# A transformer block on eight cores: one stage's loop reordered by engine, its stores moved to another queue

## What is computed

```python
x = x + attn_a(ln(x))   # delta = softplus((xn @ W0.T) @ W_delta.T + b); prefix sum of delta*B1 over the rows
x = x + ffn(ln(x))      # xn @ W_eff.T + b
x = x + attn_b(ln(x))   # softmax attention over the 8192 rows of a batch
x = x + ffn(ln(x))

# attn_a, with h = ln(x) and sums over the whole sequence:
dA = jnp.exp(delta * A1) * B1
dB = jnp.cumsum(delta * B1, axis=1)
y = dA * sum(h * Cs) + dB * sum(Cs) + residual * D
```

## Time and profile before

| what | value |
|---|---|
| time, median of 2 runs | 7493.05 us (7473.88 to 7512.21) |
| the profiled execution: time of its run | 7213.63 us |
| the profiled execution: span of its slowest core | 7211.3 us |
| spans of the 8 cores | 7192.7 to 7211.3 us |
| busy over the span | PE 61%, ACT 35%, DVE 24%, POOL 18% |
| first x2 of the stage to the last | 1416.9 to 3435.7 us |

### The profile page before, as it was taken

One profiled execution on the slowest core, in us unless ns is written; L12 is line 12 of the kernel. 1 busy time (PEld: TensorE's weight loads), 2 busy tenths in 40 slices (PEclk: granted clock), 3 DMA queues, 4 the chain that ended last, 5 costly groups with the idle time before them and its releaser, 6 DMA issues.

```text
span 7211.3 us, 65380 instructions; the slowest of 8 cores (7192.7 to 7211.3 us)
## 1 busy us (share of the span) xinstructions
PE 4364.3 (61%) x20288; PEld 1955.4 (27%) x20288; DVE 1721.1 (24%) x2744; ACT 2500.9 (35%) x4418; POOL 1323.4 (18%) x611
## 2 busy tenths in 40 slices
PE   3788887122222222222679997998899855555555
PEld 1333333000000010010334443444444322222222
DVE  0222222122222222222002221332233122222221
ACT  0555554133333333333323332333333222222222
POOL 2222222444444444444000000000000000000000
PEclk9899998565656555555889999999999977777777
DMA  4222222422222111111211110221122111111110
GB/s 124 100 99 96 95 97 76 123 72 71 74 70 75 64 60 61 53 60 35 75 42 40 55 59 30 82 94 59 53 88 94 47 35 41 41 41 43 47 41 25
DMA packets 183210, 475.80 MB, mean 66 GB/s; under 512 B 51149, under 2 KB 51278, under 8 KB 182868
## 3 DMA queue, kind: packets, MB, share of 16 engines
q1 hardware_dynamic: 98740, 295.19, 13.0%
q10 hardware_dynamic: 84128, 176.45, 6.3%
HBM read 295.12 MB, written 176.42 MB: 65 GB/s over the span
## 4 chain that ended last, share of the span: by engine, by line
PE 49%; ACT 17%; DVE 12%; POOL 11%; issue 5%; DMA 3%; ACTq 1%; DVEq 0%; POOLq 0%; SPq 0%
PE PC L1026 13%; PE PA L933 6%; PE PB L933 6%; PE PB L712 5%; PE PA L873 4%; PE PB L892 3%; DVE st L191 3%; PE PA L420 3%; PE PC L1075 3%; PE PT L186 2%; POOL p2F L670 2%; POOL p2H L723 2%; POOL p2D L673 2%; POOL g_bf L451 2%; ACT L208 2%
## 5 line engine op out<-in xcount | busy, mean ns | idle before, releaser
L1026 PE MATMUL PC<-v_res,pt_sb 128*128 128x512 bf16 x4096 | 994.9, 405 | 285.7 <-ACT pt_sb L1013 280.4
L1087 POOL TENSOR_TENSOR s_out<-zs,x3b 128x1024 f32<-128x1024 f32 x32 | 75.0, 2342 | 3694.9 <-DVE zs L1082 3694.9
L186 PE MATMUL PT<-s_id,xn2b 128*128 128x128 bf16 x512 | 64.7, 306 | 1119.6 <-ACT xn2b L212 1119.6
L1026 PEld LDWEIGHTS PC<-v_res,pt_sb 128*128 128x128 bf16 x4096 | 416.5, 103 | 813.1 <-issue 411.8
L933 PE MATMUL PA<-kT_res,qT_t 128*128 128x512 bf16 x2048 | 470.7, 384 | 28.4 <-ACT P_bf L970 22.5
L933 PE MATMUL PB<-kT_res,qT_t 128*128 128x512 bf16 x2048 | 462.9, 379 | 0.0
L186 PEld LDWEIGHTS PT<-s_id,xn2b 128*128 128x128 bf16 x512 | 49.5, 137 | 1174.7 <-issue 1174.7
L712 PE MATMUL PB<-W_eff,xn2T 128*128 128x512 bf16 x1024 | 345.1, 511 | 1.6 <-DVE p2G L720 1.5
L451 POOL TENSOR_TENSOR g_bf<-delta_f,s_B1bc 128x1024 bf16<-128x1024 f32 x64 | 150.0, 2344 | 796.2 <-ACT delta_f L442 796.2
L723 POOL TENSOR_TENSOR p2H<-p2G,p2F 128x1024 f32<-128x1024 f32 x64 | 149.6, 2337 | 758.5 <-DVE p2G L720 758.5
L933 PEld LDWEIGHTS PA<-kT_res,qT_t 128*128 128x128 bf16 x2048 | 201.5, 99 | 277.5 <-issue 42.9
(11 more groups left out here) (164 smaller groups left out, 6837.3 us busy)
## 6 DMA issues: line engine op xcount, KB each, us to landing
sc_z<-zs ACTq DMA_DIRECT2D x96, 512.0 KB, 4.6
zl<-sc_z SPq DMA_DIRECT2D x96, 512.0 KB, 4.9
xb<-x SPq DMA_DIRECT2D x64, 512.0 KB, 3.5
sc_delta<-delta_f ACTq DMA_DIRECT2D x64, 512.0 KB, 2.7
sc_res<-res_f ACTq DMA_DIRECT2D x64, 512.0 KB, 2.6
p2A<-x SPq DMA_DIRECT2D x64, 512.0 KB, 4.9
p2B<-sc_delta SPq DMA_DIRECT2D x64, 512.0 KB, 5.1
p2C<-sc_res SPq DMA_DIRECT2D x64, 512.0 KB, 6.0
```

The costliest lines, as they stand in the source:

```text
L186: e.transpose(o, i_, s_id[:, :]),
L1026: mpv = sch.add("tensor", lambda e, jj=j, nn=n, pp=p: e.matmul(PC[:, nn * 512:(nn + 1) * 512], pt_sb[pp][:, jj, :], v_res[:, jj * 1024 + n ...
```

## The change

Four things are done in stage 4; nothing outside it is touched, and the arithmetic stays.

- In `p2A` the multiplication for the exponential, and the exponential, come ahead of the multiplication for the prefix sum.
- `p2B` is split: `p2Bmm` has the matmuls and the bias, `p2Bx2` the addition x2. `p2Bx2` gets a wait for the LayerNorm of two tiles before, whose store had covered it.
- Both stores of `p2C` go from ScalarE's queue to SP's, and the first gets a wait for the normalization.
- The loop's body is put in another order, and before the loop tile 0 is transposed ahead of the LayerNorm of tile 1.

```diff
@@ p2A
+                mei = sch.add("gpsimd", lambda e, pp=p: e.tensor_mul(
+                    D_[pp][:, :], B_[pp][:, :], s_A1bc[:, :]),
+                    (VD(mk2[("ldl", i)]), GM(mr2) if i == 0 else None), inc=("g", 1))
+                mk2[("eIn", i)] = mei
+                mev_ = sch.add("scalar", lambda e, pp=p: e.activation(
+                    E_[pp][:, :], D_[pp][:, :], AF.Exp), (GM(mei),), inc=("s", 1))
                 mg0 = sch.add("gpsimd", lambda e, pp=p: e.tensor_mul(
                     g0b[pp][:, :], B_[pp][:, :], s_B1bc[:, :]),
-                    (VD(mk2[("ldl", i)]), TM(mk2.get(("tri", i - 2), 0)),
-                     GM(mr2) if i == 0 else None), inc=("g", 1))
+                    (TM(mk2.get(("tri", i - 2), 0)),), inc=("g", 1))
...
@@ p2B
-            def p2B(i):
+            def p2Bmm(i):
...
+            def p2Bx2(i):
...
                 mx2 = sch.add("gpsimd", lambda e, pp=p, qq=q3: e.tensor_add(
                     H_[pp][:, :], G_[qq][:, :], F_[qq][:, :]),
-                    (VM(mx2a), mk2.get(("sx2", i - 2))), inc=("g", 1))
+                    (VM(mx2a), mk2.get(("sx2", i - 2)),
+                     SM(mk2.get(("ln3", i - 2), 0))), inc=("g", 1))
...
@@ p2C
-                mk2[("sxn3", i)] = dma("scalar", sc_xn3[i, :, :], xn3b[p][:, :], ch=f"sx3{p}")
+                mk2[("ln3", i)] = mxn3
+                mk2[("sxn3", i)] = dma("sync", sc_xn3[i, :, :], xn3b[p][:, :],
+                                       (SM(mxn3),), ch=f"sx3{p}")
                 if i < NQ:
-                    mk2[("sx2", i)] = dma("scalar", sc_x2[i, :, :], H_[p][:, :],
+                    mk2[("sx2", i)] = dma("sync", sc_x2[i, :, :], H_[p][:, :],
...
@@ the loop
             p2Bln(0)
+            p2Btp(0)
             p2Bln(1)
-            p2Btp(0)
             p2Btp(1)
-            p2B(0)
+            p2Bmm(0)
+            p2Bx2(0)
             for i in range(NT):
-                p2C(i)
+                if i + 1 < NT:
+                    p2Bmm(i + 1)
                 if i + 3 < NT:
                     p2loads(i + 3)
                     p2A(i + 3)
+                if i + 1 < NT:
+                    p2Bx2(i + 1)
                 if i + 2 < NT:
                     p2Bln(i + 2)
                     p2Btp(i + 2)
-                if i + 1 < NT:
-                    p2B(i + 1)
+                p2C(i)
```

More of the change, by code:

```diff
@@ L660, in p2A @@
                 mk2[("tri", i)] = mtr
[L661 to L665, removed]
                 mydb = sch.add("vector", lambda e, pp=q3, PD_=PD: e.tensor_mul(
@@ L722, in p2B @@
                 mk2[("x2a", i)] = mx2a
+            def p2Bx2(i):
+                p = i % 2
+                q3 = i % 3
+                mx2a = mk2[("x2a", i)]
                 mx2 = sch.add("gpsimd", lambda e, pp=p, qq=q3: e.tensor_add(
                     H_[pp][:, :], G_[qq][:, :], F_[qq][:, :]),
-                    (VM(mx2a), mk2.get(("sx2", i - 2))), inc=("g", 1))
+                    (VM(mx2a), mk2.get(("sx2", i - 2)),
+                     SM(mk2.get(("ln3", i - 2), 0))), inc=("g", 1))
                 mk2[("x2", i)] = mx2
```

## The result

| | before | changed |
|---|---|---|
| median of all runs | 7278.8 us (22 runs) | 7362.1 us (24 runs) |
| lowest run | 7209.8 us | 7269.1 us |
| profiled execution, slowest core | 7211.3 us | 7277.1 us |

The ratio of the changed kernel to the one before is **1.0084, with a 95% interval of 1.0049 to 1.0118**: 0.8% slower, 61 us of 7210. Many runs of both kernels had cores at a lower TensorE clock and took up to 7512 and 7612 us; the ratio leaves them out, and the two runs of before from which I took the scale of my prediction, 7474 and 7512 us, were such runs.

What follows compares the result with a forecast made beforehand. Waiting, not a full engine, was taken to bound stage 4. 1433.9 + 32 x 33.6 + 28 x 32.8 + 40.2 = 3468 against 3443, 25 us more: 7239 us profiled, 7518 on the median's scale; range 7440 to 7650.

Steps and rivals of the forecast that it cites:

- the ring: Stage 4's cycle of waits that sets the time per tile: 32.65 us before, forecast 33.6 then 32.8 us.
- rival A: Stores on SP hold nothing up, loads come in time: 22.5 us a tile, 6593 or 6873 us; chance 0.07.
- the sum: Stage 4's predicted times added up: 33.6 us for 32 iterations, 32.8 for 28, plus ends; 25 us more.
- the signs named ahead: Per iteration SP waits about 30 us, GpSimd some 16, ScalarE near 10 before the exponential; x2 waits for nothing.
- step 1, "the loads": From xn3b's end to p2B's landing on SP's queue: issued at 2.1 or 1.7 us, landed at 7.7 or 6.9.
- Steps 2 and 3: Step 2, p2B's landing to L675: 10.92 us after 0.1 to start; step 3, L675 to xn3b's end: 14.87 us.
- The ends: Before and after the loop: first L679 at 1433.9 against 1435.6 us, last L679 to stage end 40.2 against 48.8.
- the last sum: The 25 us difference carried unscaled onto the 7493 us median of the runs shown, giving 7518 us.
- B: Stores and loads share SP's queue, p2B lands 7.5 us after issue: 150 us slower, 7364 or 7643; chance 0.12.
- The small step beside GpSimd: In step 3, one-column L210 is held by x2 on GpSimd, adding 0.08 us.
- the 16 us that it might have cost: If L666 were also caught beside GpSimd: 0.26 us an iteration, 16 us in all; forecast took it as free.

## Why the prediction came out as it did

**What was right.** The direction of the small difference and its mechanism. The loads of tile i+3 wait on SP behind the store of xn3b(i-1), and the ring runs through them: 1740 us of SP's waiting, the move back to ScalarE worth 630 us, and 11.2 us a tile when only the stores are moved. What the new order gives was priced under rival A: 22.5 us a tile if the loads came in time. With the loads ahead it is 22.67. The new order alone took 9.3 us a tile off, where I had about 10 for it. That nothing of the matmuls stays on the ring, that x2 waits for nothing, and that L666, not GpSimd, now releases L673 (8.56 us from L644, 8.42 in the sum) hold too. So do the signs named ahead: SP waits 31 us in the mean, GpSimd 16.7, ScalarE 10.4 before the exponential.

**Where the size was off.** The sum had 25 us more; the profiles have 66, the ratio 61. The term is step 1, "the loads". I had `p2B` issued at 2.1 us and landing at 7.7; it is issued at 2.69 and the multiplication starts at 8.4. In the first half 0.6 us of the miss is the issue: a small load behind two stores and a load takes 0.88 us of SP where the issues in the rows of before took 0.33 or 0.34. Some 0.2 is landing, 5.8 us in the mean of that half on the slowest core (6.0 in the median), where I had 5.6; on the other seven the mean was 5.2 to 5.6, so there the landing was not mis-sized. In the second half the issue came 0.1 earlier than summed, and the landing was 5.5 in the mean (5.7 in the median) where I had 5.2. Steps 2 and 3 add 0.15 and 0.18. Together the slowest core's halves are 34.8 and 33.3 us a tile where I had 33.6 and 32.8: 32 x 1.2 + 28 x 0.5 = 52 us, and 25 + 52 = 77 against the 75 by which the stage grew. The ends were right: 40.2 us from the last L679 (3473.8) to the last store (3514.0), 40.2 in the sum. The two numbers for landing stood in the range's bounds (4.6 to 7.5), the slow issue did not: the rows of before have no load behind two stores.

**Where the time was off.** The range 7440 to 7650 us does not hold 7362. The step that failed is the base of the last sum, "the median of the runs shown is 7493 us": it came from two runs 3.9% above the profiled execution, and with 22 runs the median is 7279, 214 us less. The 36 us by which the difference was too small would not have left the range: moved down by 214 us it is 7226 to 7436 and holds 7362. That the difference was not scaled is not what failed; 3.9% of 25 us is 1. I took 20 us for the spread of the runs, from these same two, where the 22 lie between 7210 and 7512. On the scale of the profiled execution, 7213.6 and near the fastest, my number was 7239 and the measured one 7279.

**A wrong sentence in step 2.** "Swapping the two costs about 0.9 us here" leaves out the other side. In the old order the exponential's input comes second, and L673 could start only 10.0 us after the first multiplication by the same rows (4.96 + 2.49 + 2.55), not 8.4. The run with the old order shows it: L644 to L673 is 9.94 us against 8.56, so with the loads late the swap gains 1.4 us a tile. The sum had the new order right, so the number did not suffer.

**The rivals.** A was wrong for this kernel and right for the one with the loads ahead. B, a landing of 7.5 us, did not come, though a pair of cores in step reached 7.0 with a store less on the queue. The small step beside GpSimd: L210 beside x2 took 0.30 us in place of 0.16, 0.14 more and not 0.08. L666 ran 0.25 us beside L670 (2014.24; L670 from 2012.15 to 2014.49) and took its usual 1.23, so the 16 us that it might have cost did not come. The Trainium skill, page "SBUF — State Buffer", section "Who interferes with whom", says that a VectorE instruction with two SBUF inputs contends with a GpSimd one that reads SBUF. L683 above, which has two SBUF inputs, agrees at 3.37 us in place of 1.28.

## What to carry to other kernels

Before a DMA is moved to another queue, list what stands behind it there and who waits for that. A store that waits for the end of an iteration, put ahead of the loads of the next, turns prefetching into a round trip, even on a queue that idles most of the time. If it must go there, emit each set of loads an iteration earlier, ahead of it (that alone was worth 9% here, 7269 to 6601 us). A change of many edits that moves the time by 1% may be a gain of 8% and a loss of almost 10% (7209 to 6634, 6634 to 7269): run its parts alone. And a base for a forecast wants more than two runs; here two gave 7493 us where 22 gave 7279.

## What the runs showed of the hardware that I had not expected

- The issue of a DMA on SP mostly takes 0.23 to 0.46 us. Behind xn3b's store, x2's store and a 512 KB load, all issued within 1.4 us, it took 0.85 to 0.99 in the changed kernel, and 0.73 to 1.06 with x2's store on ScalarE's queue. Behind one store and two 512 KB loads within the same 1.4 us it took 0.28 to 0.38. What makes the difference is open.
- Two neighbouring cores whose loads of `p2B` are issued within 1.2 us of each other, by their own time axes, have it landing at 6.3 to 7.0 us in three profiled executions; the same two 5 to 7 us apart, 4.6. In step they can stay so through half the stage and longer. That cost some 75 us in one of the two executions of that kernel, and nothing where the loads were issued an iteration ahead.
- A VectorE operation of 1.28 us with two inputs in SBUF took 3.37 beside one GpSimd operation of 2.34, and 3.0 to 3.4 in 30 of the 64 tiles of that core.
